# Layer 0's projections, linear attention and shared expert written out as one block, its weighted answers summed in layer 1's norm

## What is computed

```python
# mixer: linear attention, 16 heads of 8
qkv = (x @ qkv_w.T + qkv_b).reshape(B, Q, 3, H, hd)
k = _layernorm(k, kn_g, kn_b)          # over the 8 values of a head
v = _layernorm(v, vn_g, vn_b)
kv = einsum('bhqd,bhqe->bhde', k, v) / Q * temperature + attn_bias
att = einsum('bhqd,bhde->bhqe', q, kv) + x
return gelu(att @ p1_w.T + p1_b, approximate=False) @ p2_w.T + p2_b + x
# feed-forward: two of eight routed experts, and a dense (shared) one
weights_E = (one_hot * expert_values[..., None]).sum(axis=2)
moe_out = einsum('bse,bsed->bsd', weights_E, all_outputs)
return x + _mlp(x, sh_w1, sh_b1, sh_w2, sh_b2) + moe_out   # gelu, tanh form
```

## Time and profile before

| | us |
|---|---|
| median of three runs | 2233.63 |
| lowest, highest | 2227.62, 2236.07 |
| the profiled execution's own time | 2244.5 |
| its span, first to last instruction | 2242.7 |
| busy in it: PE, DVE, ACT, POOL | 1857.9, 1376.4, 1181.8, 463.4 |

### The profile page before, as it was taken

How to read it: one execution, slowest core, us unless ns; L and a number is a source line. 1 busy time by engine, 2 the same in 40 slices (tenths; PEclk the granted TensorE clock), 3 DMA queues, 4 the chain that set the end, 5 groups by cost and what they waited for, 6 DMA issues and landing times. The chain is left out here.

```text
span 2242.7 us, 46369 instructions
## 1 busy us (share of the span) xinstructions
PE 1857.9 (83%) x16582; PEld 1235.5 (55%) x16582; DVE 1376.4 (61%) x4008; ACT 1181.8 (53%) x2454; POOL 463.4 (21%) x544
## 2 busy tenths in 40 slices
PE   3433898846958999999999999999794389999988
PEld 3222797643946555565565555565684144445457
DVE  4678222464245677777777777776564567777525
ACT  1122454324534777777777777776133216666643
POOL 0055353025450122212110000000264300000000
PEclk9965998967978999999999999999897559999979
DMA  3141675105854000000000000010585223233001
GB/s 133 51 124 39 220 264 178 38 4 173 286 202 109 18 11 14 11 11 14 11 9 2 1 2 2 1 31 28 188 274 179 71 83 121 72 96 110 7 1 38
DMA packets 121117, 180.98 MB, mean 81 GB/s; under 512 B 16440, under 2 KB 76960, under 8 KB 120448
## 3 DMA queue, kind: packets, MB, share of 16 engines
q1 hardware_dynamic: 109552, 150.76, 20.9%
q0 software_dynamic: 10912, 22.53, 3.0%
q10 hardware_dynamic: 432, 4.79, 0.5%
HBM read 68.97 MB, written 45.72 MB: 51 GB/s over the span
## 5 line engine op out<-in xcount | busy, mean ns | idle before, releaser
L1952 ACT ACTIVATE t_p<-t_p,t_low 128x512 f32<-128x512 f32 x512 | 370.5, 724 | 199.0 <-DVE t_low L2018 199.0
L2018 DVE CUSTOM_DVE_ANT_0 t_p<-bank,L_skewed 128x512 f32<-128x512 f32 x512 | 333.2, 688 | 202.2 <-PE bank L1837 201.5
L2370 ACT ACTIVATE alibi_p<-pair 128x1024 f32<-128x1024 f32 (+1 forms) x192 | 168.1, 884 | 134.5 <-PE pair L2257 134.2
L1854 PEld LDWEIGHTS pair<-ident,t_p 64*128 64x128 f32 x4096 | 168.6, 139 | 79.0 <-issue 60.7
L2429 DVE CUSTOM_DVE_ANT_0 alibi_junk<-bank,alibi_later 128x512 bf16<-128x512 f32 (+1 forms) x256 | 150.5, 622 | 64.7 <-PE bank L2269 61.9
L2112 POOL COPY t_wide<-t_inverse 128x512 f32<-128x512 f32 x64 | 39.4, 616 | 708.3 <-DVE t_inverse L2034 708.3
L1854 PE MATMUL pair<-ident,t_p 64*128 64x64 f32 x4096 | 178.2, 224 | 1.7 <-ACT t_p L1952 0.3
L1837 PE MATMUL bank<-t_k_hi,t_q_hi 64*128 64x512 f32 x512 | 140.0, 539 | 3.4 <-DVE t_low L2018 3.4
L1804 PE MATMUL pair<-t_hT,L_wo 64*128 64x512 f32 x256 | 134.2, 604 | 0.9 <-DVE t_hT L2041 0.8
L2269 PE MATMUL bank<-alibi_k_aug,alibi_q_aug 32*128 32x512 f32 (+1 forms) x256 | 102.2, 519 | 34.1 <-DMA alibi_k_aug<-aug_k 16.3
L1800 PE MATMUL bank<-L_wv,xnT 64*128 64x512 f32 x240 | 125.5, 603 | 0.0
(11 more groups left out here) (560 smaller groups left out, 4591.3 us busy)
## 6 DMA issues: line engine op xcount, KB each, us to landing
L0moe_w<-L_packed SPq DMA_DIRECT2D x43, 578.0 KB
L2moe_w<-L_skewed SPq DMA_DIRECT2D x43, 450.0 KB, 3.0
L1moe_w<-L_packed SPq DMA_DIRECT2D x27, 578.0 KB, 3.5
alibi_q_aug<-aug_q SPq DMA_DIRECT2D x8, 1024.0 KB, 7.5
alibi_k_aug<-aug_k SPq DMA_DIRECT2D x8, 1024.0 KB, 7.7
L_skewed<-bias_table SPq DMA_DIRECT2D x16, 448.0 KB, 9.4
slots<-g ACTq DMA_DIRECT2D x3, 1560.0 KB, 9.7
L0shared_rows<-answers SPq DMA_DIRECT2D x8, 512.0 KB, 4.3
```

Of the source, the lines that this page charges most:

```text
L1854: ins = nc.tensor.transpose(turn_ps[r][:, at:at + HALF], p[rows[r], u % RING, j * P:(j + 1) * P], k.ident[rows[r], rows[r]])
L1952: nc.scalar.activation(p[:, u % RING, :], p[:, u % RING, :], ACT.Exp, bias=low[:, u % 16:u % 16 + 1], scale=-1.0, accum_out=sums[:, n % 2, ...
L2018: nc.vector.tensor_tensor_reduce(out=p[:, u % RING, :], in0=score_ps[h][:], in1=skewed[:, (n % PAIRS) * 2 + h, start:start + SEQ], scale=- ...
L2370: nc.scalar.activation(p[:, u % P_RING, :, 0:w], flip_ps[u % 2][:, :, 0:w], ACT.Exp).then_inc(expd, 1)
```

## The change

Layer 0's projections, linear attention and shared expert become one block, `mixer_block`, written out batch by batch without loops. The means of the groups of eight are taken out of the weights and the bias once (`centre_weights`), so the keys and values come out centred. The shared expert's weights are fetched in the routing block. POOL's scatter and SP's other fetches stand beside the new block. `shared_block` goes; the weighted answers are summed in layer 1's norm, which has x + b2 + dense in `k.g` already (`based`): ACT scales the first answer in its ring buffer, POOL adds it to `k.g`, DVE adds the second.

```diff
@@ norm_block, POOL @@
+                def first_half(b):
+                    pool.wait_ge(half_scaled, b + 1)
+                    nc.gpsimd.tensor_tensor(tiles(k.g, b), tiles(k.g, b), rows[:, b % RING, :, 0, :], ALU.add).then_inc(half_sum, 1)
+
+                if based:
+                    first_half(0)
                 for b in range(NB):
+                    if based and b + 1 < NB:
+                        first_half(b + 1)
                     pool.wait_ge(scaled, b + 1)
...
@@ norm_block, ACT @@
-                    ins = nc.scalar.activation(k.g[:, tile, :], rows[:, b % RING, t, 0, :], ACT.Identity,
+                    first = rows[:, b % RING, t, 0, :]
+                    ins = nc.scalar.activation(first if based else k.g[:, tile, :], first, ACT.Identity,
                                                scale=k.share[:, 0, tile:tile + 1])
...
@@ route_block @@
+        if loads:
+            @block.sync
+            def _(sp):
+                fetch(k, sp, *loads)
...
-def shared_block(k, name, chunks, func, w1, w2, b1, b2, xn, stage):
...
-def project_block(k, name, channel, token):
...
-def linear_attention_block(k, qT, kv, c, beside=None):
...
+def mixer_block(k, c, dense, beside):
...
+        kv_ps, q_ps, sum_ps, up_ps = k.banks[0:2], k.banks[2], k.banks[3], k.banks[4]
+        wide_up_ps, wide_down_ps = k.banks[5:7], k.banks[7]
...
+            def kv_product(b):
+                if b == 0:
+                    pe.wait_ge(centred_w, 1)
+                for j in range(2):
+                    if b >= 1:
+                        pe.wait_ge(kv_taken, 2 * (b - 1) + j + 1)
+                    for t in range(2):
+                        at = b * SEQ + (2 * j + t) * P
+                        ins = nc.tensor.matmul(kv_ps[j][:, t * W:(t + 1) * W], k.xnT[:, at:at + P], c["wkv"], start=True, stop=True)
+                    ins.then_inc(kv_made, 1)
...
+            def attend(b):
+                pe.wait_ge(kvb_made, b + 1)
+                pe.wait_ge(q_taken, b + 1)
+                nc.tensor.matmul(q_ps[:], kvb[:, b % 2, :], qT[:, b % 2, :], start=True, stop=True).then_inc(attended, 1)
+
+            def up(b):
+                pe.wait_ge(att_made, b + 1)
+                if b >= 1:
+                    pe.wait_ge(stored, b)
+                nc.tensor.matmul(up_ps[:], c["p1"], att[:, b % 2, :], start=True, stop=True).then_inc(up_made, 1)
+
+            def down(b):
+                pe.wait_ge(hidden, b + 1)
+                for t in range(TPS):
+                    ins = nc.tensor.matmul(up_ps[:, t * P:(t + 1) * P], hT[:, b % 2, t * P:(t + 1) * P], c["p2"],
+                                           start=True, stop=True)
+                ins.then_inc(out_made, 1)
...
+            def wide_down_chunk(b, c):
+                n = b * CHUNKS + c
+                pe.wait_ge(wide_hidden, n + 1)
+                if c == 0 and b >= 1:
+                    pe.wait_ge(added, b)
...
+            q_product(0)
+            kv_product(0)
+            for i in range(NB + 1):
+                last, live, ahead = i - 1, i < NB, i + 1 < NB
+                if i >= 1:
+                    sum_kv(last)
+                if live:
+                    wide_up_chunk(i, 0)
+                    wide_up_chunk(i, 1)
+                if i >= 1:
+                    attend(last)
+                if ahead:
+                    kv_product(i + 1)
+                if live:
+                    wide_down_chunk(i, 0)
+                    wide_up_chunk(i, 2)
+                    wide_down_chunk(i, 1)
+                if i >= 1:
+                    up(last)
+                if ahead:
+                    q_product(i + 1)
+                if live:
+                    wide_up_chunk(i, 3)
+                    wide_down_chunk(i, 2)
+                if i >= 1:
+                    down(last)
+                if live:
+                    wide_down_chunk(i, 3)
...
+            store_q(0)
+            for i in range(NB + 1):
+                last, live, ahead = i - 1, i < NB, i + 1 < NB
+                if live:
+                    square(i)
+                    wide_gelu(i, 0)
+                    wide_gelu(i, 1)
+                    take_root(i)
+                if i >= 1:
+                    gelu(last)
+                if live:
+                    wide_gelu(i, 2)
+                if ahead:
+                    store_q(i + 1)
+                if live:
+                    wide_gelu(i, 3)
...
+            def centre_weights():
+                for w, m in ((c["wkv"], w_mean), (c["bkv"], b_mean)):
+                    by_group = w.rearrange("p (g e) -> p g e", e=8)
+                    link(V.tensor_reduce(m[:], by_group, AX.X, ALU.add))
...
+            def take_kv(b):
+                for j in range(2):
+                    dve.wait_ge(kv_made, 2 * b + j + 1)
...
+            def finish(b):
+                dve.wait_ge(out_made, b + 1)
...
+            def base(b):
+                link(V.tensor_tensor(tiles(k.g, b), tiles(c["xn"], b), b2.unsqueeze(1).to_broadcast([P, TPS, P]), ALU.add))
+
+            def add_dense(b):
+                dve.wait_ge(wide_down, (b + 1) * CHUNKS)
...
+            dve.wait_ge(k.slots_zeroed, 16 * SLOT_FILLS)
+            ready(k, dve, stage)
+            centre_weights()
+            for i in range(NB + 1):
+                last, live = i - 1, i < NB
+                if live:
+                    take_kv(i)
+                if i >= 1:
+                    kv_scale(last)
+                if live:
+                    base(i)
+                    variance(i)
+                if i >= 1:
+                    residual(last)
+                    add_dense(last)
+                if live:
+                    scale(i)
+                if i >= 1:
+                    finish(last)
+
+        beside(block)
...
@@ layer0, layer1 @@
-        project_block(k, "L0proj", [(wT[:, 0:P], bq[:], 1.0, qT)], (wT[:, P:3 * P], bkv[:], kv))
-        linear_attention_block(k, qT, kv, dict(gamma=gamma[:], beta=beta[:], temp=temp[:], bias=bias[:], xn=xn,
...
+        mixer_block(k, dict(wq=wT[:, 0:P], wkv=wT[:, P:3 * P], bq=bq[:], bkv=bkv[:], gamma=gamma[:], beta=beta[:], temp=temp[:],
...
-    shared_block(k, "L0shared", 4, ACT.Gelu_apprx_tanh, w1, w2, b1, b2, xn, 5)
...
-        norm_block(k, "L1norm", True, w["wr"], k.logits, rows[:, :, 0:P])
+        norm_block(k, "L1norm", True, w["wr"], k.logits, rows[:, :, 0:P], top=2, based=True)
```

More of the change, by code:

```diff
@@ L500, in _, with route_block @@
                 route(NB - 1)
-def route_block(k, name, logits, bias, top, kind, rows, layer, table=None, keep_x=False):
+def route_block(k, name, logits, bias, top, kind, rows, layer, table=None, keep_x=False, loads=None):
     nc, T, E = k.nc, k.NT, EXPERTS
@@ L913, in _ @@
             answer(n_tiles - 1)
-def shared_block(k, name, chunks, func, w1, w2, b1, b2, xn, stage):
[L919 to L985, removed]
-                dve.wait_ge(k.got[b], arrived[b])
-                for j in range(2):
-                    if j == 0:
-                        dve.wait_ge(dense, b + 1)
-                    else:
-                        dve.wait_ge(half_sum, b + 1)
-                    for t in range(TPS):
-                        tile = b * TPS + t
-                        g = k.g[:, tile, :]
-                        ins = nc.vector.scalar_tensor_tensor(g, rows[:, b % RING, t, j, :], k.share[:, j, tile:tile + 1], g,
-                                                             ALU.mult, ALU.add)
-                    ins.then_inc(summed if j else half_sum, 1)
@@ L1276, in linear_attention_block @@
[L1276 to L1294 removed]
+        st = Stage(k, "mixer", ctx)
@@ new lines, in mixer_block @@
+        wide_up, wide_hidden, wide_down, added = (st.sem(n) for n in ("wide_up", "wide_hidden", "wide_down", "added"))
+        cen, sq = st.sb("cen", [P, 2, TPS, W]), st.sb("sq", [P, 2, TPS, W])
+        mean, rstd = st.sb("mean", [P, 2, NG]), st.sb("rstd", [P, NG])
+        root, newton = st.sb("root", [P, 2, NG]), st.sb("newton", [P, NG])
+        w_mean, b_mean = st.sb("w_mean", [P, 2 * HEADS]), st.sb("b_mean", [P, 2 * HEADS])
+        qT, kvb = st.sb("qT", [P, 2, SEQ]), st.sb("kvb", [P, 2, P])
@@ L1343, in finish @@
-            def finish(link, b, par):
-                dve.wait_ge(outm.sem, outm.at(b))
-                s = tiles(k.s, b)
-                link(V.tensor_tensor(s, out_ps[par][:].rearrange("p (t d) -> p t d", d=P), tiles(c["xn"], b), ALU.add))
-                V.tensor_tensor(s, s, c["p2_b"].unsqueeze(1).to_broadcast([P, TPS, P]), ALU.add).then_inc(stored.sem, 1)
-            with dve.Fori(0, NB // 2) as g:
-                link = Link(dve, chain, g * LINKS)
-                for stage in (centre, variance, scale, kv_scale, residual, finish):
-                    for par in range(2):
-                        stage(link, g * 2 + par, par)
-                assert link.n == LINKS
@@ new lines, in variance, with scale @@
+            def variance(b):
```

(12 more changed lines are left out.)

245 lines of the change are left out of this document (97 added, 148 removed).

## The result

The changed kernel took 2180.66 us in the median of four runs, the kernel before 2230.62 beside it: a ratio of 0.9773 with a 95% interval of 0.9754 to 0.9792. The forecast was 2185 in a range of 2164 to 2210, faster. Its profiled execution took 2184.86 us (span 2183.0).

The account below looks back on a forecast made before the run. Layer 0's stages ran one after another, each filling a different engine, with TensorE waiting 77.9 us for normed keys. Block -12, shared expert -62, layer 1's norm +25 sum to -49: 2185 us from 2233.63, range 2164 to 2210.

Parts of the forecast that it names:

- The round: One batch's turn of the new mixer block, set by the written order across TensorE, ScalarE and VectorE: 16.1 us.
- VectorE's 7.1: VectorE's work per mixer-block batch outside scale, seven 128x512 instructions, variance and kv_scale: 7.1 us.
- the ring: Mixer block's closed chain of waits: TensorE to up, ScalarE's gelus and load, TensorE's down, VectorE's finish to dense sum; 16.1 us.
- The block: Layer 0's new mixer block: 138 us against 150.6 for projections and attention, so -12.
- The fourth table load: ScalarE in the mixer block: whether Square needs another 1.28 us load each batch was left undecided.
- The price of a switch: ScalarE's table switches in the mixer block: 1.3 us each and no more; the skill's 2.66 would give 2199.
- The scatter: POOL's scatter beside the mixer block: from 80.5 to 196, covered by the block, next limit capping the gain at 34.
- Layer 1's norm: Layer 1's norm takes over the weighted sum: POOL's gated additions 4.4 us apart, root at 41, +25 in all.
- the 2 us: End of layer 1's norm: the last 24 filler transposes start cold and end some 2 us later.
- The low clock: Rival, mixer block: TensorE's clock stays low throughout, round 26 us, 80 us more, 2265; chance 0.06.
- VectorE alone at 13.1: Rival, mixer block: VectorE alone sets the round at 13.1 us, 2163 after the scatter's cut; chance 0.12.
- layer 1 at layer 3's pace: Rival, layer 1's norm: it runs as fast as layer 3's norm, 13 us less, 2172; chance 0.12.

Follow-up runs that it names:

- down first: Changed kernel with the last batch's down product issued before wide_down 2 on TensorE; 2177.12 us, ratio 0.9755 to the kernel before.
- one gelu: Changed kernel with the mixer's exact gelu replaced by the dense expert's tanh form, one table load less a batch; 2175.06 us, ratio 0.9741 to the kernel before.
- spare table: Changed kernel with a short constant Sqrt added on ScalarE behind wide_gelu 3, two more table loads a batch; 2184.71 us, ratio 0.9797 to the kernel before.
- two ahead: Changed kernel with layer 1's norm scaling and adding the first answer two batches ahead instead of one; 2184.74 us, ratio 0.9799 to the kernel before.
- more filler: Changed kernel with five instead of three sets of filler transposes per collected batch in layer 1's norm; 2187.59 us, ratio 0.9811 to the kernel before.
- sum on VectorE: Changed kernel with VectorE instead of POOL adding the scaled first answer in layer 1's norm; 2174.36 us, ratio 0.9733 to the kernel before.
- no dense work: Changed kernel without the dense expert's products, gelus and sum in the new block; 2159.20 us, ratio 0.9674 to the kernel before.
- down first with filler: Changed kernel with down before wide_down 2 and five sets of filler transposes in layer 1's norm; 2177.11 us, ratio 0.9762 to the kernel before.
- joined: Changed kernel with down before wide_down 2, first answers summed two batches ahead and five filler sets; 2175.12 us, ratio 0.9765 to the kernel before.

## Why the prediction was right, step by step

**The round.** Forecast 16.1, measured 15.23. The path was the one that was written: 3.9 to the end of up (148.0 to 151.9), 2.7 on ScalarE, 2.1 on TensorE. The mis-sized term is VectorE's 7.1: it took 6.4 to 6.5 (156.75 to 163.2). I gave all seven instructions of 128x512 their own 0.69 and 0.03 of hop; two that don't depend on each other start 0.60 apart (161.94, 162.54). The 0.3 for semaphores was 0.1. VectorE's wait in finish, forecast 2.6, is 2.65; down first, one gelu and the spare table show that it is the ring's slack.

**The block.** Forecast 138, with its end at 218; measured 131.3, at 211.4. Six rounds of 0.87 are 5.2 of the 6.7 missing. The first keys were normed at 97.1, where 79.8 + 17.9 was forecast; the second batch took 11.4 for 11.7 and the tail 11.5 for 12. This first profile shows the shortest block of the six with rounds of 15.2 us. In the other five (the changed kernel again, two ahead, spare table, more filler, sum on VectorE) the last round took 16.88 or 16.89 us, and the stage to the experts' first load 134.5 to 135.5. So against the 151.6 and 152.9 of before the block's usual gain is 16 to 18 us, where 12 were forecast. No run puts the centring or the loops back, so what each part of the rewriting brings by itself is not shown. The fourth table load, left open, doesn't come: ScalarE's groups show 25 loads in the block, eight for Sqrt, eight for Gelu, nine for the tanh form, and none at Square:

```profile
L1288 ACT ACT_TABLE_LOAD x9 | 11.5, 1283 | 0.2
...
L1275 ACT ACT_TABLE_LOAD x8 | 10.3, 1283 | 0.1
L1281 ACT ACT_TABLE_LOAD x8 | 10.3, 1283 | 0.1
L1269 ACT ACTIVATE mixer_sq<-mixer_cen 128x1024 f32<-128x1024 f32 x8 | 8.5, 1058 | 28.7 <-DVE mixer_cen L1328 28.7
```

The price of a switch was taken as its load, against the Trainium skill (ScalarE: Activation LUTs, What ACT_TABLE_LOAD costs), by which it would be 2.66 us. In the ring, where one gelu took a switch away, it was worth 1.33 us a round: the measurement decides for the load alone.

**The scatter.** Forecast from 80.5 to 196; it ran from 80.9 to 190.8, and what waits for it came some 7 us later (no dense work). Covered, as stated, and the next limit, as stated.

**The shared expert.** Forecast -62; the stretch is gone and the experts' stage is as long as before: 159.6 and 159.0 us against 221.1 and 220.8.

**Layer 1's norm.** Forecast: gated additions 4.4 us apart, root at 41, +25 in all. Measured 4.33, 41.0 and 74.1 - 49.5 = +24.6. Up to the root the step was right in mechanism and size; sum on VectorE shows the mechanism. Behind the root the 2 us had the wrong cause: the last filler was to start cold and end later. TensorE's timeline and two windows near the logits, which start at 429.49:

```profile
416.74 1.04 PE L148 MATMUL bank<-ident,L1t_rows 128*128 128x128 f32 x8
```

```profile
425.00:427.00 2.00, 2.00 (x15) 0.65 0.00 0
427.00:429.00 2.00, 2.00 (x11) 0.50 0.00 0
```

The first turns started 3.7 us behind the root, where before it was 4.0, so the filler cost nothing; the 1.4 us more to the logits (16.5 for 15.1) came as the clock fell over the last products. Nor is it a fixed price: root to logits took 14.8 to 20.9 us in the profiles of changed kernels, with the clock and the start of the turns.

**The sum.** -49 was forecast. The stages show -56 and -52, the block's share of it -19.3 and -18.4 where -12 was forecast; the medians show -50. That the median came so near to 2185 is in part luck: the block gave more than was forecast, and stretches that weren't forecast at all took some of it back. Which these are in the unprofiled runs, no trace can show.

**The rivals.** The low clock didn't come (1.00 in the block); without the dense work it does fall (0.74), so in this block the dense products kept it up. VectorE alone at 13.1 is not reached, as the written order was the bound; layer 1 at layer 3's pace neither, as POOL's order held it.

## What to carry to other kernels

Where no engine is full, find the ring of waits that closes on itself and price each link from rows: an instruction costs its time only if it stands on the ring, so moving one line (down ahead of wide_down 2) was worth what dropping a table load was, and two more loads off the ring cost the round nothing. Work that is handed to the next stage has to be priced in that stage's own ring and by what runs beside it on POOL. Read small changes from the stage in the trace, since the rest of the program moved by more than they did.

## What the runs showed of the hardware

TensorE's granted clock fell from 1.00 to 0.50 while TensorE was busy in all of each window, in layer 1's transposes and 8-column products: in both profiles of the changed kernel and in one gelu, two ahead, no dense work, spare table, down first with filler and joined; in more filler it fell over the last 2 us. It stayed up to the logits in both profiles of the kernel before, in down first, in sum on VectorE and in these two together. The Trainium skill (TensorE: Matmul & The Clock Gate, The HAM clock gate) lets it fall behind idle time; these windows have none. What tells the two apart stays open.

In the last round of the block, where TensorE waits 2.3 us for the dense sum, the clock dipped in the changed kernel's second profile and not in its first, which has the same wait. It dipped in the four other profiles with rounds of 15.2 us and in one gelu too, and in none of the four with down first. Windows of TensorE in the second:

```profile
192.00:196.00 4.00, 1.96 (x9) 0.77 0.06 21
196.00:200.00 4.00, 4.00 (x15) 0.81 0.00 0
```

It made the round 1.65 us longer. The last stretch of layer 3, from its first load of the bias queries, took 456.5 to 473.9 us in the twelve profiles of the changed kernel and its variants, none of which touches it.
